# A chunked state-space mixer with seven-level decays: two levels per stationary load, sources sorted through DRAM

## The reference

```python
proj = xn @ in_proj_w.T                       # gate 512 | x 512, B 128, C 128 | dt 64
xBC = silu(conv_b + sum(conv_w[:, i] * xp[:, i:i + l, :] for i in range(4)))
dt = softplus(dt + dt_bias);  A = -exp(A_log)
# per head h (64 heads of 8 channels), state of 128, time t, source s <= t:
y[t] = sum_s (C[t] . B[s]) * exp(sum_{s<r<=t} dt[r] A) * dt[s] x[s]   +  D * x[t]
hg = y * silu(gate)
s = (hg * rsqrt(mean(hg * hg) + 1e-5) * norm_w) @ out_proj_w.T
g = silu(experts(xn))                         # top-1 of 8 by sigmoid(xn @ router_w)
out = x + s * g
```

## Time and profile before

| | us |
|---|---|
| median of 3 runs | 532.98 (532.93 to 533.37) |
| the profiled execution, its own time | 533.9 |
| its span, first to last instruction | 532.1 |
| TensorE busy | 460.3 (87%) |
| VectorE busy | 373.2 (70%) |
| GpSimd busy | 287.2 (54%) |
| ScalarE busy | 183.0 (34%) |
| mean granted TensorE clock | 0.922 of full |

### The profile page before, as it was taken

The page is one execution under the profiler, slowest core; times in us unless marked ns, Lnnn a source line. Parts: engine busy times, 40 slices in busy tenths (PEclk is TensorE's granted clock), DMA queues, the critical chain, the costliest instruction groups (busy, mean ns, idle before and its releaser), DMA issues.

```text
span 532.1 us, 7288 instructions
## 1 busy us (share of the span) xinstructions
PE 460.3 (87%) x2270; PEld 335.1 (63%) x2271; DVE 373.2 (70%) x804; ACT 183.0 (34%) x401; POOL 287.2 (54%) x267
## 2 busy tenths in 40 slices
PE   1777488779999989997989999997959999999980
PEld 1763146566878777966667799985436666666650
DVE  5407799999979999869999898993324455454540
ACT  1551645232235433342323423211413344434420
POOL 3100749783689459766458589980223434434440
PEclk9999679787999979998969999998989999999995
DMA  8996210000000000000000000394971332332225
GB/s 278 284 175 69 90 70 2 1 0 11 1 11 11 12 0 12 11 20 1 1 0 12 12 11 11 53 340 165 366 235 49 92 97 83 87 106 79 70 61 177
DMA packets 27176, 42.10 MB, mean 79 GB/s; under 512 B 2980, under 2 KB 19880, under 8 KB 26952
## 3 DMA queue, kind: packets, MB, share of 16 engines
q1 hardware_dynamic: 23432, 30.53, 20.3%
q0 software_dynamic: 3712, 11.17, 6.7%
HBM read 31.42 MB, written 14.47 MB: 86 GB/s over the span
## 4 chain that ended last, share of the span: by engine, by line
PE 64%; DVE 20%; DMA 4%; issue 4%; ACT 4%; SPq 2%; POOLq 0%; POOL 0%; DVEq 0%; ACTq 0%
PE BANK L930 12%; PE BANK L866 12%; PE BANK L947 7%; DVE ARENA L986 7%; DVE ARENA L1146 7%; PE BANK L818 7%; PE BANK L895 5%; PE BANK L879 3%; PE BANK L792 3%; DMA ARENA<-in_w_down 3%; PE BANK L886 2%; PE BANK L899 2%; PE BANK L848 2%; PE BANK L829 2%; PE BANK L939 2%
## 5 line engine op out<-in xcount | busy, mean ns | idle before, releaser
L514 POOL TENSOR_TENSOR ARENA<-ARENA 128x512 f32<-128x512 f32 x112 | 142.8, 1312 | 5.6 <-issue 4.4
L866 PEld LDWEIGHTS BANK<-ARENA 128*128 128x128 f32 x768 | 93.0, 201 | 12.8 <-DVE ARENA L1165 7.6
L866 PE MATMUL BANK<-ARENA 128*128 128x64 f32 x768 | 93.2, 283 | 7.2 <-DVE ARENA L1165 7.2
L818 PE MATMUL BANK<-ARENA,W_MAIN 128*128 128x512 f32 x160 | 79.8, 650 | 12.3 <-DVE ARENA L1165 11.4
L930 PE MATMUL BANK<-ARENA 128*128 x184 | 84.7, 604 | 1.6 <-ACT ARENA L738 1.4
L986 DVE TENSOR_TENSOR ARENA<-ARENA 128x256 f32<-128x256 f32 (+9 forms) x102 | 67.6, 664 | 3.1
L818 PEld LDWEIGHTS BANK<-ARENA,W_MAIN 128*128 128x128 f32 x160 | 31.8, 209 | 50.4 <-issue 29.8
L573 POOL DMA_INDIRECT final_rows<-ARENA x23 | 24.2, 1052 | 65.8 <-DVE ARENA L986 65.8
L930 PEld LDWEIGHTS BANK<-ARENA 128*128 128x128 f32 x184 | 35.5, 194 | 37.5 <-issue 36.4
L1146 DVE SCALAR_TENSOR_TENSOR ARENA<-BANK,CONVC,ARENA 128x511 f32<-128x511 f32 (+2 forms) x72 | 53.5, 746 | 6.0 <-ACT ARENA L648 4.1
L986 DVE TENSOR_TENSOR BANK<-BANK,ARENA 128x256 f32<-128x256 f32 (+1 forms) x112 | 52.4, 468 | 2.7
(11 more groups left out here) (130 smaller groups left out, 718.2 us busy)
## 6 DMA issues: line engine op xcount, KB each, us to landing
ARENA<-in_w_gate SPq DMA_DIRECT2D x8, 512.0 KB, 9.2
ARENA<-in_w_up SPq DMA_DIRECT2D x8, 512.0 KB, 9.8
ARENA<-in_w_down SPq DMA_DIRECT2D x8, 512.0 KB, 10.2
ARENA<-x_by_expert SPq DMA_DIRECT2D x23, 129.0 KB, 3.1
mixer_rows<-ARENA SPq DMA_DIRECT2D x16, 128.5 KB, 2.1
ARENA<-in_x SPq DMA_DIRECT2D x4, 512.0 KB, 6.2
mixer_rows<-in_x SPq DMA_DIRECT2D x1, 2048.0 KB
out_dram<-final_rows SPq DMA_DIRECT2D x4, 512.0 KB, 5.9
```

Of the source, the lines that this page charges most:

```text
L514: nc.gpsimd.tensor_tensor(out=XS[par][:, slot, :].rearrange("p (a h) -> p a h", a=HD), in0=E2[par][:, slot, :].unsqueeze(1).to_broadcast([ ...
L818: ins = nc.tensor.matmul(bank[:, :], lhsT=W_MAIN[:, k, i * P:(i + 1) * P], rhs=XNT[:, k, t * GW:(t + 1) * GW], start=(k == 0), stop=(k == ...
L866: ins = nc.tensor.matmul(bank[:, at:at + 64], lhsT=XS[par][:, lev - 1, blk * P:(blk + 1) * P], rhs=odd(GM[par][:, lev - 1, :], lev), start ...
```

## The change

The levels are done in three pairs, (0, 1), (2, 3), (4, 5), and level 6 by itself (`TOP`). For a pair, the 64 sources of one level (bit 0) and the 64 of the other are put on 128 partitions, so that one stationary load serves both; the moving operand has 128 target columns, 64 of each level, and the mask keeps those of the same level. Level 0 becomes a level like the others. To bring sources to their partitions, ACT writes x and dt into slot `SUF` of `XS`, SP stores this slot as rows in DRAM (`source_rows`) and loads each pair's rows back in two halves. B and C are sorted along their columns by ACT, 12 copies a group (`sort`), and three more C.B products are made from them. The reach sums of a level's targets are made for two tiles in one product (in `pair`, with `DAR` of both tiles stationary), and ACT moves each half to the partitions where it is needed (`spread`); `ET` has four buffers. `mid` takes six chunks of ring `d`. SP now has a list of steps as well, and expert loads 0 to 3 are issued one after another from `head` of tile 13 on. Below, the core of the diff; constants, buffers and semaphore names are left out.

```diff
-                for slot in range(XSLOTS):
-
-                    if t > 1:
-                        chunk = slot // 2 if slot < SUF else NEW
-                        pool.wait_ge(d_moved, d_of("mid", t - 2, chunk))
-                    nc.gpsimd.tensor_tensor(
-                        out=XS[par][:, slot, :].rearrange("p (a h) -> p a h", a=HD),
-                        in0=E2[par][:, slot, :].unsqueeze(1).to_broadcast([P, HD, HEADS]),
-                        in1=XT[par].rearrange("p (a h) -> p a h", a=HD), op=ALU.mult).then_inc(x_scaled, 1)
+                if t > 1:
+                    pool.wait_ge(d_moved, d_of("mid", t - 2))
+                scaled(slice(0, 64), TOP, SUF)
+
+                pool.wait_ge(rows_in[par], 16 * 2 * PAIRS * (t // 2 + 1))
+                nc.gpsimd.tensor_tensor(
+                    out=E2[par][:, 0:PAIRS, :], in0=E[:, 0:PAIRS, par, :], in1=XS[par][:, 0:PAIRS, DIN:],
+                    op=ALU.mult).then_inc(e2_ready, 1)
+                pool.wait_ge(e2_ready, 2 * t + 2)
+                for j in range(PAIRS):
+                    scaled(slice(0, P), j, j)
+                pool.wait_ge(x_scaled, t * XSLOTS + 1)
+                scaled(slice(0, P), SUF, SUF)
```

```diff
+            def sort_rows(t):
+
+                par = t % 2
+                sp.wait_ge(a_moved, a_of("head", t))
+                sp.dma_start(xr_dram[t], XS[par][:, SUF, :]).then_inc(rows_out, 16)
+                sp.wait_ge(rows_out, 16 * (t + 1))
+                for j in range(PAIRS):
+                    if t > 1:
+                        sp.wait_ge(d_moved, d_of("mid", t - 2, 1 + j))
+                    for half in range(2):
+                        rows = xr_dram[t].rearrange("(q o m) c -> q o m c", o=2, m=1 << 2 * j + half)[:, 0, :, :]
+                        sp.dma_start(XS[par][half * 64:half * 64 + 64, j, :], rows).then_inc(rows_in[par], 16)
...
+                    def spread(columns, source):
+                        for c in range(2):
+                            for r in range(2):
+                                ins = nc.scalar.activation(ET[(t + c) % 4][r * HEADS:(r + 1) * HEADS, columns],
+                                                           source[c * HEADS:(c + 1) * HEADS, :], ACT.Exp)
+                        ins.then_inc(a_moved, 1)
+
+                    spread(slice(0, 64), bank[:, 2 * P:2 * P + 64])
+                    act.wait_ge(a_written, a + 3)
+                    spread(slice(64, 64 + DIN), bank_of_a(a + 2)[:, :])
...
+                        act.wait_ge(scattered, 16 * TILES)
+                    nc.scalar.activation(XS[par][:, SUF, DIN:], heads_of(DT, t), ACT.Copy)
                     act.wait_ge(a_written, a + 1)
-                    nc.scalar.activation(XT[par], bank_of_a(a)[:, :], ACT.Copy).then_inc(a_moved, 1)
-
-                    act.wait_ge(gd_ready, 2 * t + 2)
+                    nc.scalar.activation(XS[par][:, SUF, 0:DIN], bank_of_a(a)[:, :], ACT.Copy).then_inc(a_moved, 1)
...
+                    bank = bank_a(a)
+                    for slot in range(4):
+                        ins = sums(bank, slot * P, CONST[:, C_SUM + slot, :], da, P)
+                    ins.then_inc(a_written, 1)
+                    bank = bank_a(a + 1)
+                    sums(bank, 0, CONST[:, C_SUM + SUF, :], da, P)
+                    sums(bank, P, CONST[:, C_ONE, :], da, P)
+                    sums(bank, 2 * P, da, CONST[:, C_REACH + 4, 0:64], 64).then_inc(a_written, 1)
+                    sums(bank_a(a + 2), 0, da, CONST[:, C_REACH:C_REACH + 4, :].rearrange("p m t -> p (m t)"),
+                         4 * P).then_inc(a_written, 1)
...
+                    pe.wait_ge(bc_sorted, q + 1)
                     bank = bank_d(d)
-                    nc.tensor.matmul(bank[:, 0:P], lhsT=XBC[q % 2][:, HB, cols_of(t)],
+                    for j in range(PAIRS):
+                        nc.tensor.matmul(bank[:, j * P:(j + 1) * P], lhsT=BC[:, 0, j, t % GT, :],
+                                         rhs=BC[:, 1, j, t % GT, :], start=True, stop=True)
+                    nc.tensor.matmul(bank[:, PAIRS * P:], lhsT=XBC[q % 2][:, HB, cols_of(t)],
...
+                    pe.wait_ge(d_moved, d_of("head", t))
+                    bank = bank_d(d)
+                    pe.wait_ge(x_scaled, t * XSLOTS + 1)
+                    for blk in range(HB):
+                        ins = nc.tensor.matmul(bank[:, blk * 64:(blk + 1) * 64],
+                                               lhsT=XS[par][0:64, TOP, blk * P:(blk + 1) * P],
+                                               rhs=GM[par][0:64, TOP, 64:], start=True, stop=True)
+                    ins.then_inc(d_written, 1)
+                    for j in range(PAIRS):
+                        bank = bank_d(d + 1 + j)
+
+                        pe.wait_ge(x_scaled, t * XSLOTS + 2 + j)
                         for blk in range(HB):
-                            at = ((lev - 1) % 2) * HB * 64 + blk * 64
-                            ins = nc.tensor.matmul(bank[:, at:at + 64], lhsT=XS[par][:, lev - 1, blk * P:(blk + 1) * P],
-                                                   rhs=odd(GM[par][:, lev - 1, :], lev), start=True, stop=True)
-                        if lev % 2 == 0:
-                            ins.then_inc(d_written, 1)
+                            ins = nc.tensor.matmul(bank[:, blk * P:(blk + 1) * P],
+                                                   lhsT=XS[par][:, j, blk * P:(blk + 1) * P],
+                                                   rhs=GM[par][:, j, :], start=True, stop=True)
+                        ins.then_inc(d_written, 1)
...
+                    scale(0)
+                    scale(1)
+                    add(LEVELS - 1)
+                    extra(0)
+                    add(0)
+                    scale(2)
+                    add(1)
+                    extra(1)
+                    add(2)
+                    scale(3)
+                    add(3)
+                    extra(2)
```

More of the change, by code:

```diff
@@ L71, with times @@
 FACTORS = LOG1P_DEGREE // 2
+def times(lev, bit):
+    return [t for t in range(P) if (t >> lev) & 1 == bit]
 def constant_matrices():
     k, t = np.arange(P)[:, None], np.arange(P)[None, :]
[L78 to L88, removed]
+    within, masks, reach = [], [], []
+    for j in range(PAIRS):
+        lev = np.repeat([2 * j, 2 * j + 1], P // 2)
+        source, target = (np.array(times(2 * j, bit) + times(2 * j + 1, bit)) for bit in (0, 1))
+        within.append((k >> lev == source >> lev) & (k > source))
+        masks.append((lev[:, None] == lev) & (source[:, None] >> lev + 1 == target >> lev + 1))
+    top = LEVELS - 1
+    within += [(k >> top == t >> top) & (k > t), k > t]
+    masks.append((k >> top == 0) & (t >> top == 1))
+    for lev in [*range(1, LEVELS), LEVELS, 0, 0]:
+        of = np.arange(P) if lev == LEVELS else np.array(times(lev, 1))
+        reach.append((k >> lev == of >> lev) & (k <= of))
+    mats = [k == t, *within, k >= 0 * t, k < t, *masks, *np.split(np.concatenate(reach, axis=1), 5, axis=1)]
     return np.stack([m.astype(np.float32) for m in mats], axis=1)
@@ L135, in schedule @@
     first = [("conv", 0, i) for i in ORDER]
-    steps = first[:3] + [("rank", 0, 0)] + first[3:] + [("flush", 0, ORDER[-1]), ("pair", 0, 0), ("head", 0, 0),
+    steps = first[:3] + [("rank", 0, 0)] + first[3:8] + [("sort", 0, 0)] + first[8:] + [
+        ("flush", 0, ORDER[-1]), ("pair", 0, 0), ("head", 0, 0),
                                                         ("turn", 0, 0)]
@@ L233, in mixer_moe_kernel @@
         BT = [part(P) for _ in range(2)]
-        XT = [part(DIN) for _ in range(2)]
         O = [part(OW) for _ in range(2)]
@@ L656, in act_step @@
                     if t > 0:
[L657 to L664 removed]
+                        act.wait_ge(e2_ready, 2 * t)
@@ L884, in pe_step @@
                     pe.wait_ge(x_scaled, (t + 1) * XSLOTS)
-                    pe.wait_ge(a_moved, a_of("turn", t, 1))
-                    nc.tensor.matmul(bank[:, :], lhsT=BT[par], rhs=XS[par][:, SUF, :], start=True,
+                    pe.wait_ge(a_moved, a_of("turn", t))
+                    nc.tensor.matmul(bank[:, :], lhsT=BT[par], rhs=XS[par][:, SUF, 0:DIN], start=True,
                                      stop=True).then_inc(d_written, 1)
```

265 lines of the change are left out of this document (127 added, 138 removed).

## The result

| | before | with the change |
|---|---|---|
| median, us | 532.95 (4 runs) | 546.39 (4 runs, 544.42 to 549.58) |
| profiled execution, span | 532.1 | 545.1 |

The ratio is 1.027, 95% interval 1.024 to 1.029. The forecast was 513 (500 to 526).

A forecast was written before the change was run, and what follows sets the result against it. The prediction took PE to bound six mixer steps, DVE six others, and PE, POOL and DVE three more. Terms -10.0, -12.3, -1.5 and +3.5 sum to -20.3, giving 513 us from a median of 532.98; range 500 to 526.

The forecast's parts named there:

- the last lands 3.1 later, 5.0. I take 8.7, as the loads are nearest to the 129 KB row: Trip through DRAM: store 3.8, six issues 1.9, last load landing 3.1 later, together 8.7 us.
- Nothing is put on the expert phase: Expert phase: no change in time, experts 0 to 3 being issued earlier, one after another behind the row trips.
- the start: Before the first tile's middle: sorting, exponentials and trip delay DVE's first add; +3.5 us (0 to +7).
- DVE-bound steps: Six mixer steps with most of the convolution: DVE work falls, -2.05 us each after a returned stall, -12.3 in all.
- last tiles: Three steps without convolution and the last tile's middle, with exponentials in the loop: together -1.5 us (-6 to +3).
- Rival 3: The DRAM trip enters the two-tile loop: at 18 us, queued behind other transfers, +15 and 548 us; chance 0.09.
- The loop: State, copy, trip, scalings and adds close over two tiles: 23.0 us, 11.5 a step, hidden in PE-bound and DVE-bound steps.
- PE-bound steps: Six mixer steps with PE full: wider level products and a smaller turn save 1.66 us each, -10.0 in all.
- DVE's new stall for ScalarE's first pass: DVE-bound steps: DVE waits for ACT to issue the convolution's first pass; 0.5 us a step.
- Rival 1: More is hidden: carry operations speed up as POOL works less, start costs nothing, plain steps reach 10.3; 501.5 us, chance 0.17.
- Rival 2: Six chunks on the same five banks tie PE to DVE, losing +6 and +4 us of gain; 523, chance 0.25.
- Rival 4: Half-row records or reading a DMA-written tile price no lower per matmul, PE gains only the turn; about 520, chance 0.04.

The follow-up runs named there:

- run 5: The changed kernel with the sources of levels 4 and 5 in position-major order, so their row loads have 16 and 32 rows outermost; 527.0 us.
- run 9: The changed kernel with only level 5's sources in position-major order, level 4 still loaded in 4 blocks of 16 rows; 531.4 us.
- run 10: The changed kernel, sources in its own order, with level 4's row loads issued as four loads each and level 5's as two; 527.5 us.
- run 1: The changed kernel with the loads of experts 0 to 3 all issued behind the row trip of tile 15; 538.6 us.
- run 11: The changed kernel with levels 4 and 5 in position-major order and all loads of experts 0 to 3 behind tile 15's row trip; 521.7 us.
- run 4: The changed kernel with expert loads behind tile 15's row trip and every head step ahead of the same tile's pair step; 542.8 us.
- run 8: The changed kernel with expert loads behind tile 15's row trip and the rows' transposes and copy one tile earlier, in four buffers; 519.6 us.
- run 7: The changed kernel with late expert loads, POOL waits per pair, levels 4 and 5 position-major, and rows' transposes and copy a tile earlier; 505.9 us.

## Why the prediction was wrong

**The step that failed** is "the last lands 3.1 later, 5.0. I take 8.7, as the loads are nearest to the 129 KB row". The 129 KB load of the earlier trace rows spreads over 128 partitions on both sides. The row loads of levels 4 and 5 have 4 and 2 blocks as the outer dimension of their source, and the last of them landed 6.3 us after its issue: 9.8 for the six loads instead of 5.0, 12.2 for the trip instead of 8.7. I had read the bytes off the row, not the shape. Run 5 puts the landing at 2.3 us and the trip at 8.8 when these two sources have 16 and 32 rows outermost. That this is my number is luck: store 2.4 (3.8 forecast), issues 4.1 (1.9), landing 2.3 (3.1). Runs 9 and 10 show that it follows the number of blocks, and not the order of the rows. The Trainium skill (DMA: Bandwidth & Descriptors, "Why a DMA increments its semaphore by 16 and not by 1") states the rule: a transfer runs on the largest number of engines up to 16 that divides the outermost dimensions of both sides. Two engines for level 5 and four for level 4 agree with the 1 and 2 tenths of 16 and the 53 and 105 GB/s of the change's trace. That rule spoke against this change, and I had passed it by.

**"Nothing is put on the expert phase"** was right of that phase and wrong of what the sentence goes on to say, that the expert loads are issued "behind the row trips": they are ahead of the next trip. The store of tile 15 waited 11.5 us behind expert 1's loads and the rows of tile 14. Putting them last gave 7.8 and 5.3 us (runs 1 and 11). With both the shape and the experts cured (run 11) the kernel takes 521.7, faster than before and still 8.7 above the forecast: of these, 4.0 lie in the start and the DVE-bound steps (-4.8 for -8.8) and 2.4 in the last tiles (+0.9 for -1.5). Rival 3 had named this ("behind other transfers") and put its trip at 18; I gave it 0.09, on the ground that the queues are empty outside the start and the expert loads. The tiles in which the trip is hidden least are the ones with the expert loads.

**The loop.** Its form held. Where the trip is 9 us, the store of tile 15 follows that of tile 13 by 23.3 us (run 11, 302.85 and 326.19), against 23.0 forecast; that of tile 14 follows that of tile 12 by 26.8, against 26.0 with the 3 us of the exponentials. In the change it is 28.7 and 32.1. Rival 3's arithmetic held less well: by its half a microsecond per step and one at the start, 12.2 us of trip leave a gain of some 11, and the kernel lost 13. The trip also cost 10 us in the DVE-bound stretches, which I had called hidden. 5.0 of them lie in the first step (23.2 us, 18.2 without the trip), and they are tile 0's own trip: DVE's first add waits for the Y that POOL makes behind it, and comes at 103.57 us, 98.57 without the trip.

```profile
103.57 0.42 DVE L1058 TENSOR_TENSOR ARENA<-ARENA,BANK 128x256 f32<-128x256 f32 x1 [2.10 <-POOL ARENA L568]
```

The other 5 are spread over the later steps, and I can't lay them to one wait.

**Term by term**, with what the change measured and what it measures without the trip:
- PE-bound steps: -10.0 forecast, -9.2 and -8.9. Right; wide records are 0.12 apart (24 in 2.94 us).
- DVE-bound steps: -12.3 forecast, -4.1 and -14.1. This has to be read with the start, since the first stretch begins at tile 0's first level product, and what that moved back left the stretch for the start. The two together: -8.8 forecast, +2.6 and -8.5. So the sum was right without the trip, but one part of it was not. I had put DVE's new stall for ScalarE's first pass at 0.5 a step, 3.0 in all; without the trip DVE waits 12.3 us for it in the mixer, for 0.9 before. Against that its work fell by more than the 2.55 a tile reckoned: up to tile 12's first level product it is busy for 221.3 us instead of 261.2, 3.3 a tile. The two misses cancel, which is luck.
- Last tiles: -1.5 forecast, +19.4 and -9.1. With a trip of 9 us and the experts out of the way it is +0.9.
- Start: +3.5 forecast (the working gives 101.3 - 97.40, 3.9). By the stretches it is +6.7 and +5.6, and 4.4 of that are the pair's exponentials ahead of the copy: run 4 takes them away (91.6 to 87.2) and pays elsewhere. But the forecast was for another event, DVE's first add, at 97.40 before: it comes at 103.57 in the change (+6.2), 99.38 in run 5 (+2.0) and 98.57 without the trip (+1.2). There the trip is 5.0 of the 6.2.

One more sum was off: by rival 3's prices a trip of 6.7 us would lower the forecast by 5 (1 on each of three steps, 2 at the start), not by some 3.

**The rivals.** Rival 1's first mechanism shows, for one group of the two. In the change the carry operations of the second group took 0.17 us each at 87.5 to 88.4, where POOL was idle, waiting for rows (85.6 to 96.6). Those of the fourth took 1.12 to 1.19 at 238.3 to 241.8, where POOL was scaling, as before the change (1.13 to 1.20). Rival 2's is visible (PE waits 17 to 18 us for the convolution's last multiply) and cost no more than was allowed, since the run without the trip has that wait and -8.5 of the -8.8 above. Rival 4 is out by the PE stretches.

## What to carry to other kernels

Price a DMA by its shape before its bytes: look at the outermost dimension of each side, and take for comparison only a transfer whose outer dimensions are as wide. Here the row gathers of few large blocks were the slow ones; reordering them, or issuing each block by itself, took the loss away (527.0 and 527.5). When a change puts a round trip into a loop, ask where it has least cover, and look at what else is queued exactly there; then begin the trip earlier before making it shorter, since run 8 gained as much as run 5 with the slow loads left as they were, at the price of four more buffers. The two add up: with both, waits per pair and late experts the kernel takes 506.

## What the runs showed of the hardware

- A load of 147 KB from 2 blocks of 32 rows of 2304 B ran at about 50 GB/s (the changed kernel, 307.3 to 309.4 us), one from 4 blocks at about 100 (306.3 to 307.2 there, beside the other; without it 61 to 123 at the end of the trip in run 9). With 16 rows or more outermost both disappear in traffic that mostly runs at 100 to 300 GB/s (run 5).
- Issuing loads took SP about 0.6 us each for sources of separate blocks (six in 3.56, four in 2.40), 0.46 for neighbouring rows (six in 2.76, run 10), 0.33 for the 288 KB store. I had taken 0.32 for all.
- A store of 288 KB was confirmed in 2.1 us on an idle queue, no longer than one of 128.5 KB; behind six row loads it took 7.0 (run 8), with two of the six spread 3.0 (run 7), behind one expert's loads and six row loads 11.5.
- In one and the same execution of the changed kernel, DVE operations on small SBUF tiles (128x12 and 128x6) took 0.17 us each while POOL was idle, and three of five took 1.12 to 1.19 while it worked (at 87.5 and 238.3 us).
